# One-operand one-hots and weighing in graph attention, an earlier softmax step on TensorE, edge keys loaded during routing, more one-hots made in the node network

## The reference, cut to what matters

```python
# 1: attention with 8 heads over the edges, then a node network (256 -> 1024 -> 256)
y = segment_sum(alpha * v[src], dst) @ Wp.T + bp
x1 = feat + y;  x1 = x1 + gelu(layernorm(x1) @ W1.T + b1) @ W2.T + b2
# 2: mixture of 8 experts, the best 2 for each node (256 -> 1024 -> 256)
# 3: three graph attention layers; heads x width = 4x128, 4x128, 1x256
h = x @ W
e = leaky_relu(al_s[src] + al_d[dst], 0.2)        # al = sum over the width of h * a
ee = exp(e - segment_max(e, dst)[dst])
alpha = ee / segment_sum(ee, dst)[dst]
out = segment_sum(h[src] * alpha, dst) + b
#    then a three-layer network on the nodes
# 4: a second mixture of experts like the first
```

## Time and profile before

| | |
|---|---|
| median of three runs | 4595.52 us (4590.25 to 4599.95) |
| the profiled execution | 4598.59 us, its span 4596.8 us |
| mean granted clock of TensorE, share of full speed | 0.885 |
| busy in the span: PE, DVE, ACT, POOL | 3554.1, 2729.1, 2011.7, 2115.6 us |

### The profile page before, as it was taken

One profiled execution on the slowest core, in us unless ns is written; L12 is line 12 of the kernel. 1 busy time (PEld: TensorE's weight loads), 2 busy tenths in 40 slices (PEclk: granted clock), 3 DMA queues, 4 the chain that ended last, 5 costly groups with the idle time before them and its releaser, 6 DMA issues. The chain is left out here.

```text
span 4596.8 us, 73966 instructions
## 1 busy us (share of the span) xinstructions
PE 3554.1 (77%) x19614; PEld 2768.5 (60%) x19615; DVE 2729.1 (59%) x6789; ACT 2011.7 (44%) x6612; POOL 2115.6 (46%) x2092
## 2 busy tenths in 40 slices
PE   5788887794999478888768789875767667649995
PEld 3455554683888456677545667754655444438885
DVE  4688888545122358777656878865676665671112
ACT  0588885221222138778743778775321000112221
POOL 0577774000222115777731577774277777002221
PEclk8899998995999788999989899998877776769997
DMA  2677774443777756787653678765364443115556
GB/s 72 187 229 227 229 227 130 125 145 93 261 260 261 253 222 224 235 259 228 194 159 113 239 238 276 229 195 177 137 199 145 139 121 103 49 41 202 184 181 230
DMA packets 347072, 852.48 MB, mean 185 GB/s; under 512 B 52357, under 2 KB 156396, under 8 KB 338156
## 3 DMA queue, kind: packets, MB, share of 16 engines
q0 software_dynamic: 144384, 455.22, 32.6%
q1 hardware_dynamic: 195932, 391.65, 25.3%
q10 hardware_dynamic: 6416, 1.59, 0.2%
HBM read 766.74 MB, written 81.54 MB: 185 GB/s over the span
## 5 line engine op out<-in xcount | busy, mean ns | idle before, releaser
L1833 POOL DMA_INDIRECT h<-h_table,src_of x1392 | 1428.9, 1027 | 933.6 <-PE ps L1868 440.3
L1848 PE MATMUL ps<-h,gat_layer_hot 128*128 128x261 f32 (+1 forms) x4640 | 1306.0, 428 | 380.1 <-DVE h L2081 266.9
L1848 PEld LDWEIGHTS ps<-h,gat_layer_hot 128*128 128x128 f32 x4640 | 908.7, 208 | 651.7 <-DVE gat_layer_hot L2075 203.2
L1933 ACT ACTIVATE h<-h,gat_shared 128x128 f32<-128x128 f32 x2784 | 862.9, 388 | 121.5 <-DMA h<-h_table,src_of 121.2
L728 POOL DMA_INDIRECT edges_rows<-kv_table,src_of x464 | 458.9, 989 | 270.2 <-POOLq L210 129.3
L2104 DVE TENSOR_TENSOR acc<-acc,ps 128x522 f32 (+1 forms) x696 | 422.2, 607 | 240.7 <-issue 112.4
L1010 ACT ACTIVATE acc<-ps,moe_experts_b 128x256 f32<-128x256 f32 (+1 forms) x512 | 201.5, 444 | 604.8 <-PE ps L960 604.6
L2081 DVE TENSOR_TENSOR h<-h,gat_shared 128x256 f32<-128x256 f32 (+1 forms) x696 | 354.7, 510 | 172.7 <-DMA h<-h_table,src_of 171.2
L1567 POOL DMA_INDIRECT moe_experts_rows<-normed,moe_slot_in x112 | 108.8, 971 | 644.7 <-POOLq L210 569.8
L960 PE MATMUL ps<-moe_experts_turned,moe_experts_w 128*128 128x256 f32 (+1 forms) x2048 | 402.2, 355 | 2.4 <-DMA moe_experts_w<-in_L_ffn_W 2.4
L971 PE MATMUL ps<-moe_experts_w,acc 128*128 128x256 f32 x1792 | 397.2, 379 | 1.3 <-DMA moe_experts_w<-in_L_ffn_W 1.3
(11 more groups left out here) (370 smaller groups left out, 4867.9 us busy)
## 6 DMA issues: line engine op xcount, KB each, us to landing
moe_experts_w<-in_L_ffn_W SPq DMA_DIRECT2D x128, 1024.0 KB
gat_layer_hots<-hot_table SPq DMA_DIRECT2D x174, 562.0 KB
hot_table<-acc SPq DMA_DIRECT2D x58, 562.0 KB
h<-h_table,src_of POOLq DMA_INDIRECT x1392, 2.8
edges_dst_row<-dst_rows SPq DMA_DIRECT2D x58, 256.0 KB, 4.3
acc<-src_rows SPq DMA_DIRECT2D x58, 256.0 KB, 6.0
acc<-dst_rows SPq DMA_DIRECT2D x58, 256.0 KB, 6.9
h_table<-h SPq DMA_DIRECT2D x10, 1280.0 KB
```

The lines of the kernel that those rows point to most:

```text
L1833: nc.gpsimd.indirect_dma_start(g.rows[:, r, e, 0:W], None, g.table, bass.IndirectOffsetOnAxis(ap=k.src_of[:, 2 * t + e:2 * t + e + 1], axis=0)
L1848: mm = nc.tensor.matmul(k.ps[t % S * PIECES + p][:, 0:PIECE], hot[:, t // BATCH % HOTS, t % BATCH * 2 + e, :], g.rows[:, t % RING, e, p * ...
L1933: last = act.mul(cols, cols, sums(t)[:, e, h:h + 1])
```

## The change

It has five parts.

- **proj**: all 25 denominators are clipped and inverted at the first tile, in two operations of 128x200. ACT builds the layer-normed input into `k.h`, DVE adds the bias to PE's result and then adds the two.
- **ffn0 and moe0's experts**: 39 hot batches are made in ffn0, three for each group, in three different steps; the experts make 19, in their first 19 slots.
- **Edge keys**: SP loads the keys and the attention weights in moe0's routing phase, which ends when they have landed. ACT's loads and the waits of `spare_step` are gone.
- **PE's order in the graph layers**: the softmax step of an item is called ahead of that item's sum.
- **One-hot and weighing in the graph layers**: DVE makes the one-hot for one item at a time with two `tensor_scalar` of 128x128 (12 buffers of one item instead of 3 of four), and weighs with two `tensor_scalar` of 128x128 (gat3: of 128x256) that take `alpha` as a scalar for each partition, where a `tensor_tensor` read it as a second operand.

```diff
@@ -48,7 +48,8 @@
 HOTW = 2 * 8 * P + 8 * TILES
-HOTS_FFN = 2 * -(-TILES // 2)
+HOTS_FFN = 3 * -(-TILES // 2)
+HOTS_X = ITEMS // 4 - HOTS_FFN
 
...
@@ -851,22 +853,27 @@
         v, den = nc.vector, ph.buf["den"]
-
-        c(v.tensor_scalar(den[:, slot, :], row(k.acc, t, C, C + HEADS0), 1e-30, None, ALU.max))
-        c(v.reciprocal(den[:, slot, :], den[:, slot, :]))
+        if t == 0:
+            inverted = ph.sem("inverted")
+            v.tensor_scalar(den[:], k.acc[:, :, C:C + HEADS0], 1e-30, None, ALU.max).then_inc(inverted, 1)
+            ph.dve.wait_ge(inverted, 1)
+            v.reciprocal(den[:], den[:]).then_inc(inverted, 1)
+            ph.dve.wait_ge(inverted, 2)
         return v.tensor_tensor(dst.rearrange("p (h d) -> p h d", d=HD0),
                                row(k.acc, t, 0, C).rearrange("p (h d) -> p h d", d=HD0),
-                               den[:, slot, :].rearrange("p (h o) -> p h o", o=1).to_broadcast([P, HEADS0, HD0]), ALU.mult)
+                               den[:, t, :].rearrange("p (h o) -> p h o", o=1).to_broadcast([P, HEADS0, HD0]), ALU.mult)
+
+    def normed_rows(t, ps):
+        return nc.scalar.activation(row(k.h, t, 0, C), row(k.x, t, 0, C), ACT.Identity, bias=shift[:, t:t + 1], scale=rstd[:, t:t + 1])
 
     def evac(ph, t, slot, ps, c):
-        v, feat = nc.vector, ph.buf["feat"]
-        c(v.tensor_scalar(feat[:, slot, :], row(k.x, t, 0, C), rstd[:, bass.ds(t, 1)], shift[:, bass.ds(t, 1)],
-                          ALU.mult, ALU.add))
-        c(v.tensor_tensor(feat[:, slot, :], feat[:, slot, :], ph.buf["bp"][:], ALU.add))
-        return v.tensor_tensor(row(k.h, t, 0, C), ps[0][:, 0:C], feat[:, slot, :], ALU.add)
-
-    phase_dense(k, "proj", 2, [("wp", C)], stage, 2, evac, 2,
-                sb=[("wp", [P, 2, C], F32), ("bp", [P, C], F32), ("den", [P, 2, HEADS0], F32), ("feat", [P, 2, C], F32)],
+        v, some = nc.vector, ph.buf["some"]
+        c(v.tensor_tensor(some[:, slot, :], ps[0][:, 0:C], ph.buf["bp"][:], ALU.add))
+        ph.dve.wait_ge(ph.act_taken, ready(t, 3))
+        return v.tensor_tensor(row(k.h, t, 0, C), row(k.h, t, 0, C), some[:, slot, :], ALU.add)
+
+    phase_dense(k, "proj", 2, [("wp", C)], stage, 0, evac, 1, evac_act=normed_rows,
+                sb=[("wp", [P, 2, C], F32), ("bp", [P, C], F32), ("den", [P, TILES, HEADS0], F32), ("some", [P, 2, C], F32)],
                 loads=[("wp", weights(a["L0_gnn_Wp"])), ("bp", wide(a["L0_gnn_bp"]))], norm=(k.h, 1e-5, rstd, shift))
...
@@ -910,7 +917,7 @@
         for s in range(2):
-            sp.wait_ge(self.stored[s], 16 + n // 2 * 16)
+            sp.wait_ge(self.stored[s], 16 + (n + 1 - s) // 2 * 16)
 
...
@@ -1111,11 +1118,21 @@
 
+            batches = iter(range(HOTS_FFN))
+
             def make_hots(t, slot):
-                for n in (2 * t, 2 * t + 1):
-                    hots.make(dve, n, n, n % 2)
-
-            staggered(dve, groups, [stage, turned_copy(k, f, dve, of, width), make_hots, take, stat, aggregate], unrolled=True)
+                n = next(batches)
+                hots.make(dve, n, n, n % 2)
+
+            def stat_and_make(t, slot):
+                stat(t, slot)
+                make_hots(t, slot)
+
+            def aggregate_and_make(t, slot):
+                aggregate(t, slot)
+                make_hots(t, slot)
+
+            staggered(dve, groups, [stage, turned_copy(k, f, dve, of, width), make_hots, take, stat_and_make, aggregate_and_make], unrolled=True)
             dve.wait_ge(m.aggregated, TILES)
...
@@ -1182,8 +1199,17 @@
         link, diff, exped, masked, counted, named, found = (ph.sem(s) for s in ("link", "diff", "exped", "masked", "counted", "named", "found"))
-        zeroed = ph.sem("zeroed")
+        zeroed, keys_in, w_loaded = ph.sem("zeroed"), ph.sem("keys_in"), ph.sem("w_loaded")
         block = ph.block()
+
+        @block.sync
+        def _(sp):
+            if keys:
+                parts, _ = wa_parts(k, layers, k.h)
+                load_parts(sp, parts, w_loaded)
+                keys.load(sp, keys_in)
+                sp.wait_ge(w_loaded, 48 * len(parts))
+                sp.wait_ge(keys_in, 16 * keys.count)
 
...
@@ -1474,16 +1500,16 @@
                 load_down(t, slot)
-                hots.load(sp, t + HOTS_FFN, t, slot)
+                if t < HOTS_X:
+                    hots.load(sp, t + HOTS_FFN, t, slot)
 
             def store_hots(t, slot):
-                hots.store(sp, t + HOTS_FFN, t, slot)
+                if t < HOTS_X:
+                    hots.store(sp, t + HOTS_FFN, t, slot)
 
             staggered(sp, SLOTS_X, [load_up, load_down_and_rows, None, store_hots] if keys else [load_up, load_down], unrolled=True)
             if keys:
-                hots.end(sp, SLOTS_X)
-                sp.wait_ge(keys_in, 16 * keys.count)
-                sp.wait_ge(w_loaded, 48 * len(parts))
+                hots.end(sp, HOTS_X)
 
...
@@ -1503,9 +1529,6 @@
         def _(act):
-            if keys:
-                keys.load(act, keys_in)
-                load_parts(act, parts, w_loaded)
             act.wait_ge(f.biases_turned, 1)
...
@@ -1544,9 +1568,6 @@
             def spare_step(t, slot):
-                if t == 4:
-                    dve.wait_ge(keys_in, 16 * keys.count)
-                    dve.wait_ge(w_loaded, 48 * len(parts))
                 if 4 <= t < 4 + len(span_work):
...
@@ -1753,7 +1774,7 @@
     PIECE = -(-FULL // PIECES)
-    BATCH, HOTS, NB = 4, 3, 4
+    HOTS, NB = 12, 4
     S = 6 // PIECES
...
@@ -1837,15 +1855,14 @@
             def sum_item(t):
-                if t % BATCH == 0:
-                    pe.wait_ge(marked, t // BATCH + 1)
+                pe.wait_ge(marked, t + 1)
                 pe.wait_ge(weighed, t + 1)
                 pe.wait_ge(scaled, t + 1)
                 if t >= S:
                     pe.wait_ge(added, t - S + 1)
                 for p in range(PIECES):
                     for e in range(2):
-                        mm = nc.tensor.matmul(k.ps[t % S * PIECES + p][:, 0:PIECE], hot[:, t // BATCH % HOTS, t % BATCH * 2 + e, :],
+                        mm = nc.tensor.matmul(k.ps[t % S * PIECES + p][:, 0:PIECE], hot[:, t % HOTS, e, :],
                                               g.rows[:, t % RING, e, p * PIECE:(p + 1) * PIECE], start=(e == 0), stop=(e == 1))
...
@@ -1896,14 +1913,14 @@
             for t in range(-CH, ITEMS):
+                c, n = softmax_step(t)
+                if n is not None:
+                    softmax(c, n)
                 if t >= 0:
                     sum_item(t)
                 q = scored(t)
                 if q is not None:
                     products(q)
-                c, n = softmax_step(t)
-                if n is not None:
-                    softmax(c, n)
 
...
@@ -2069,17 +2086,18 @@
                     dve.wait_ge(exped, t // CH + 1)
-                if t % BATCH == 0:
-                    if t >= HOTS * BATCH:
-                        dve.wait_ge(summed, t - (HOTS - 1) * BATCH)
-                    v.tensor_tensor(hot[:, t // BATCH % HOTS],
-                                    k.iota_row[:, 0:P].rearrange("p (a n) -> p a n", a=1).to_broadcast([P, 2 * BATCH, P]),
-                                    k.dst_in[:, 2 * t:2 * (t + BATCH)].rearrange("p (s a) -> p s a", a=1).to_broadcast([P, 2 * BATCH, P]),
-                                    ALU.is_equal).then_inc(marked, 1)
+                if t >= HOTS:
+                    dve.wait_ge(summed, t - HOTS + 1)
+                for e in range(2):
+                    last = v.tensor_scalar(hot[:, t % HOTS, e, :], k.iota_row[:, 0:P], k.dst_in[:, 2 * t + e:2 * t + e + 1], None,
+                                           ALU.is_equal)
+                last.then_inc(marked, 1)
                 dve.wait_ge(gathered[t % RING], (t // RING + 1) * 32)
-                alpha = sums(t)[:, :, 0:by_dve].rearrange("p s (h o) -> p s h o", o=1)
-                v.tensor_tensor(heads(t, 0, by_dve), heads(t, 0, by_dve), alpha.to_broadcast([P, 2, by_dve, D]), ALU.mult
-                                ).then_inc(weighed, 1)
+                for e in range(2):
+                    for h in range(by_dve):
+                        cols = g.rows[:, t % RING, e, h * D:(h + 1) * D]
+                        last = v.tensor_scalar(cols, cols, sums(t)[:, e, h:h + 1], None, ALU.mult)
+                last.then_inc(weighed, 1)
 
```

More of the change, by code:

```diff
@@ L479, in phase_dense @@
         link_s, link_e, stored = ph.sem("link_s"), ph.sem("link_e"), ph.sem("stored")
+        ph.act_taken = act_taken
         ph.fetched = [ph.sem(f"fetched{g}") for g in range(TILES // 5)]
@@ L1153, in phase_gate, with phase_route @@
                 loads=[("wg", weights(wg)), ("bg", wide(bg))], stores=tile_stores(k.normed, k.h, C))
-def phase_route(k, name, r):
+def phase_route(k, name, r, keys=None, layers=()):
     nc = k.nc
@@ L1425, in phase_experts @@
         shared_in = ph.sem("shared_in")
```

(11 more changed lines are left out.)

## The result

The change takes 4494.47 us (median of four runs, 4492.14 to 4494.85) against 4592.89 of the kernel before beside it (four runs, 4590.09 to 4599.95): a ratio of 0.9782, 95% interval 0.9765 to 0.9799, or 98 us. The profiled execution has a span of 4492.8 us, 104.0 less than before.

The account below looks back on a forecast made before the run. DVE was taken to bound proj, POOL's gathers to pace gat1 to gat3, late first product to delay moe0's experts. Terms -16 + 24 - 27 + 0 - 17 - 17 - 26 = -79 gave 4516 us, range 4484 to 4572.

Parts of the forecast that it names:

- What stretches a gather: gat1 to gat3: a two-SBUF-operand DVE operation in progress when a gather begins holds it until its end; 34 us a layer.
- the prediction's formula: Graph layers: average hold (d - 0.126)²/2/1.337 for an operation of length d, with a gather every 1.337 us.
- Rival 3: Graph layers: a run of short DVE operations holds the gather to its end, +15 us in each layer; 4622 us, chance 0.08.
- gat1 and gat2, -17 each: Graph layers gat1, gat2: an item takes 2.59 instead of 2.67 us, 232 times; 0 to -30 us each.
- rival 1: gat1, gat2: gathers get faster, layers don't, as DVE's short operations cost 0.22 us each; 4550 us, chance 0.2.
- The pitch of short operations: DVE in gat1, gat2: four short operations an item follow each other every 0.198 us; from 0.24 the change is no gain.
- gat3, -26: Graph layer gat3: gathers alone set the pace, and their excess of 37 us falls to 11; -19 to -30 us.
- ffn0, +24: ffn0 with 39 batches: the body costs nothing more, the uncovered tail ends at 1057 instead of 1033; +17 to +30 us.
- moe0's experts, -27: moe0's experts: -19.5 us from ACT's issues leaving the front, -7.6 from 13 batches fewer; -22 to -31 us.
- proj, -16: proj: a tile takes 1.51 us on DVE instead of 2.30, for 24 tiles; -13 to -20 us.
- the keys in routing, 0: moe0's routing: SP's key loads have landed by the phase's end at 1110; 0 us, up to +6 if SP is slower.
- The sum of the range's ends: Whole program: best ends of all parts together give -126 us, worst ends -25; all on one side called unlikely.

Follow-up runs that it names:

- the first experiment repeated: The changed kernel with the one-hots of 4 items made again in one two-operand operation of 1.22 us, run a second time: 4557.82 us.
- the experiment: The changed kernel with the edge keys and attention weights loaded by ACT again at the start of moe0's experts: 4516.81 us.

## Why the prediction was right, and where its steps were not

4516 us was forecast with a range of 4484 to 4572; 4494.5 was measured, against a gain of 79 one of 98 (104 in the profiles). The signs of all seven terms and the two quiet places (routing, the rest of the program) came out. By its own steps:

- **What stretches a gather: shown.** Taking the long one-hot back brings the busy time back (the first experiment repeated: +22 us in gat1, +27.5 in gat3). A gather is held by the operation in which it starts and ends 0.82 us after it (or after its own 0.946 us, if that is later), whether that has one SBUF operand or two; short ones hold too, but little is left of them. In gat1 of the kernel before 58 one-hots of 1.22 us cost 26.9 us (0.46 each) and 232 weighings of 0.42 us 8.7 (0.037 each), near the 0.447 and 0.033 of the prediction's formula; in the change all that gathers take above 0.946 us is 7.7 us. In the forecast "operations with two SBUF operands" hold; the right words are long ones whose operands are all in SBUF. DVE's adding of the sum, 700 ns with one operand in PSUM, does not hold: of the 172 gathers in gat1 and gat2 of the kernel before that began in it and in nothing else, none took more than 0.951 us. So it is in the change:

```profile
1955.12 0.70 DVE L2122 TENSOR_TENSOR acc<-acc,ps 128x522 f32 x1 [0.21 <-issue]
1955.22 0.95 POOL L1851 DMA_INDIRECT h<-h_table,src_of  x1 [0.30 <-issue]
```

  Rival 3, a run of short operations that holds a gather to its end, is out. Of the change's gathers 266 begin in a run of short operations that goes on behind the one in progress; the longest took 1.08 us. Here a gather begins in the first of four; it ends 0.82 us after that one (1950.34), while by the rival it would have ended 0.82 us after the fourth (1950.93) and taken 1.61 us:

```profile
1950.07 0.47 DVE L2092 TENSOR_SCALAR gat_layer_hot<-iota_row,dst_in 128x128 f32<-128x128 f32 x2
1950.46 0.47 DVE L2099 TENSOR_SCALAR h<-h,gat_shared 128x128 f32<-128x128 f32 x2
1950.13 1.03 POOL L1851 DMA_INDIRECT h<-h_table,src_of  x1 [0.30 <-issue]
```

  The Trainium skill's rule (SBUF — State Buffer, "SBUF: two separate sides"), that an fp32 one-operand operation in a fast mode locks the shared ports too, but only for its own instruction, agrees with these rows.

- **gat1 and gat2, -17 each: both sides priced about right, their meeting wrong (-26.4, -25.5).** The failed step compared one rate of the gathers, 2.67 us an item, with the rate of a chunk of 64 items with products and softmax, 2.59, and took the difference 232 times. The chunk came out as forecast, 2.57 (1896.1 to 2060.5), and DVE's busy time grew by the 0.17 us an item that was forecast (40.2 us over 232 items). But there the kernel before was as fast (403.5 us for 156 items in both), since it lived on the ring's lead and DVE waited for no rows: the 12 us that those items should have won did not come. In them it went as in rival 1 (gathers faster, layer not), though not by the pitch that rival 1 names. The last 76 items have no products: they go as fast as rows come, 2.26 us an item with the ring all but full at their start, where it was 2.6. For those the gathers' pace and the lead count, and both had improved. By estimate from these numbers, five more items of lead are some 13 us, and 0.14 us on each of some 70 gathered items another 10. That -17 came as near as it did is partly luck.
- **The pitch of short operations: 0.198, right on average (0.201, the median 0.196) and wrong as a constant.** The one-hot's operations took 306 ns on average and not 284, since gathers stretch some of them, see below.
- **gat3, -26: -34.4.** The hold was put at up to 18 us; the busy time of 441.88 leaves 3.0 over 464 x 0.946. The 128x256 scaling takes 0.35 us at the median and not 0.41, and a gather seldom starts in one: only 29 of the 464 gathers there took over 957 ns.
- **ffn0, +24: +26.7, by two errors.** "The third batch costs nothing in the body" was wrong: DVE stood in waits for rows when results were ready, and the last result was taken 6.3 us later (1.3 of them are PE's). The tail was put at 24 and was 20.5, since the link is 7.8 us. The errors go against each other, and the total near 24 owes something to that.
- **moe0's experts, -27: -28.4.** Undone one by one the keys are worth 14.4 and the batches 10.8, 25.2; the remaining 3 are what both cost together before. The forecast had 19.5 and 7.6, one too large and one too small; that their sum of 27 is nearly right is luck.
- **proj, -16: -16.8**; the keys in routing, 0: 0.
- **The sum of the range's ends.** From the prediction's own parts the best ends make -124 and the worst -18, where it has -126 and -25. Its range doesn't hang on them.
- **Not seen:** that the batches' move loses more in ffn0 than it wins in the experts. The numbers stood there, +24 against 7.6, and only their sum with the other parts was judged.

Open: why the eight key loads took ACT 24.8 us before the change and 20.56 in the experiment. The batches' transfers of the experts' start are in both, so what differs wasn't isolated.

## What to carry to other kernels

Where gathers are issued one after the other without a pause, the DVE operations beside them that have all operands in SBUF cost roughly by the square of their length: cut a long one that can meet a gather's start into short ones, even if DVE gets more work by it, and check first that DVE isn't then the bound. When producer and consumer run at nearly the same pace with a ring between them, test speedups of both together: here, in gat1 and gat2, the order alone brought between -3 and +2 us, the short forms alone 5 to 6, and both 26. An engine that issues without a pause doesn't yet set the pace: look also whether the one behind it waits for it. And price each part of a change on its own where it takes from one phase and gives to another; work added beside a wait costs nothing only while its own loads and stores keep up, and it needs time left behind it at the phase's end.

## What the runs showed of the hardware

The hold works the other way too, but only for operations with one operand. In the change, a one-hot `tensor_scalar` of 128x128 that starts in the first 0.4 us of an undisturbed gather takes 280 ns at the median (541 cases). One that starts 0.4 to 0.6 us into it takes 444 (226 cases), one that starts 0.6 to 0.8 us into it 333 (137); these longer ones end 0.05 to 0.11 us (medians) after the gather does. The two-operand form of the same size takes 284 to 285 wherever it starts (experiment with short two-operand one-hots, 205 and 136 cases in the same two places). That is where the mean of 306 against 286 comes from:

```profile
L2092 DVE TENSOR_SCALAR gat_layer_hot<-iota_row,dst_in 128x128 f32<-128x128 f32 x1392 | 354.7, 306 | 2.7 <-ACT gat_shared L1958 2.7
```
```profile
L2092 DVE TENSOR_TENSOR gat_layer_hot<-iota_row,dst_in 128x128 f32<-128x128 f32 x1392 | 341.7, 286 | 2.7 <-ACT gat_shared L1958 2.7
```

The same page of the Trainium skill says that whichever of the two starts first holds the ports for the whole instruction; here a gather that is under way does not lengthen an operation that starts in its first 0.4 us, nor a two-operand operation at all, so in this the measurement differs and decides.
